# One-hot columns of an edge-count build: one two-input comparison for four windows, or two scalar comparisons for each

## The reference

```python
msgs = h[edge_src]
agg = jax.ops.segment_sum(msgs, edge_dst, num_segments=n) * inv_deg     # first network
deg = jax.ops.segment_sum(ones, dst, num_segments=n)                    # second network
mean = jax.ops.segment_sum(x[src], dst, num_segments=n) / clip(deg, 1.0)
```

## Time and profile before

| | |
|---|---|
| median of three runs | 639.3 us |
| the profiled execution | 638.31 us |
| its span, first to last instruction | 636.5 us |
| TensorE busy | 591.3 us, 93% |
| VectorE busy | 243.6 us, 38% |
| ScalarE busy | 219.3 us, 34% |
| GpSimd busy | 28.7 us, 5% |

### The profile page before, as it was taken

How to read it: one execution, slowest core, us unless ns; L and a number is a source line. 1 busy time by engine, 2 the same in 40 slices (tenths; PEclk the granted TensorE clock), 3 DMA queues, 4 the chain that set the end, 5 groups by cost and what they waited for, 6 DMA issues and landing times.

```text
span 636.5 us, 9707 instructions
## 1 busy us (share of the span) xinstructions
PE 591.3 (93%) x3133; PEld 348.6 (55%) x3133; DVE 243.6 (38%) x483; ACT 219.3 (34%) x391; POOL 28.7 (5%) x35
## 2 busy tenths in 40 slices
PE   0348999999999999999999999999999999999996
PEld 0336786868677656444545545654454545444455
DVE  5569885858576751476741111110010101000000
ACT  0466665656565542254542212211111111011112
POOL 2810000000000000001110000000000000000000
PEclk9999999999999999999999999999999999999999
DMA  9303000100000000432311000030020100101011
GB/s 228 91 11 93 0 17 2 33 1 32 0 32 16 18 20 23 129 97 88 82 33 42 16 16 16 5 91 16 1 49 0 44 5 18 31 6 42 0 37 27
DMA packets 28303, 23.97 MB, mean 38 GB/s; under 512 B 4783, under 2 KB 27618, under 8 KB 28149
## 3 DMA queue, kind: packets, MB, share of 16 engines
q1 hardware_dynamic: 23740, 20.49, 12.3%
q10 hardware_dynamic: 3337, 1.80, 1.4%
q0 software_dynamic: 1200, 1.33, 0.7%
HBM read 17.41 MB, written 6.19 MB: 37 GB/s over the span
## 4 chain that ended last, share of the span: by engine, by line
PE 89%; DMA 3%; POOL 2%; DVE 2%; issue 1%; ACT 1%; ACTq 0%; SPq 0%; DVEq 0%; POOLq 0%
PE ps L818 51%; PE ps L835 22%; PE ps L853 12%; PE ps L828 2%; DMA key_d<-adj 1%; POOL adj L1146 1%; PE ps L1039 1%; POOL adj L1158 1%; POOL adj L1152 1%; DMA invc<-inv_d 1%; DMA wt_d<-adj 1%; DMA adj<-key_d,adj 1%; PE ps L1011 1%; PE ps L1357 1%; DMA adj<-in_dst_dram 0%
## 5 line engine op out<-in xcount | busy, mean ns | idle before, releaser
L818 PE MATMUL ps<-adj,hs_b 125*128 (+2 forms) x1050 | 205.7, 352 | 0.0
L818 PE MATMUL ps<-adj,hs_a 125*128 (+2 forms) x700 | 162.4, 357 | 0.0
L818 PEld LDWEIGHTS ps<-adj,hs_b 125*128 125x128 f16 x1050 | 95.6, 97 | 105.8 <-issue 9.9
L475 DVE TENSOR_TENSOR hs_b<-iota,hs_b 128x1000 f16<-128x1000 f16 (+1 forms) x175 | 130.2, 797 | 40.5 <-PE ps L853 34.8
L680 ACT ACTIVATE adj<-ps 125x500 f32 (+3 forms) x175 | 98.2, 567 | 52.3 <-PE ps L853 47.5
L853 PEld LDWEIGHTS ps<-hs_b 128*125 128x125 f16 x625 | 94.9, 204 | 35.5 <-DVE hs_b L475 9.9
L853 PE MATMUL ps<-hs_b 128*125 128x125 f16 x625 | 103.6, 298 | 4.6 <-ACT adj L680 2.3
L818 PEld LDWEIGHTS ps<-adj,hs_a 125*128 125x128 f16 x700 | 69.8, 107 | 37.0 <-issue 5.0
L665 DVE TENSOR_TENSOR hs_a<-ps,hs_a 125x512 f32<-125x512 f32 (+1 forms) x7 | 4.4, 634 | 170.3 <-PE ps L1085 170.3
L835 PE MATMUL ps<-aggT,wts 128*128 128x500 f32 (+1 forms) x112 | 44.5, 540 | 0.4 <-ACT aggT L778 0.4
L835 PE MATMUL ps<-aggT,hs_a 128*128 128x500 f32 (+1 forms) x84 | 35.1, 540 | 0.5 <-ACT aggT L806 0.5
(11 more groups left out here) (143 smaller groups left out, 341.3 us busy)
## 6 DMA issues: line engine op xcount, KB each, us to landing
invc<-inv_d SPq DMA_DIRECT2D x24, 250.0 KB, 3.4
self_d<-hs_b SPq DMA_DIRECT2D x6, 250.0 KB, 2.0
hs_b<-self_d SPq DMA_DIRECT2D x6, 250.0 KB, 3.5
hs_b<-in_x_dram SPq DMA_DIRECT2D x6, 250.0 KB
x_d<-hs_b SPq DMA_DIRECT2D x6, 250.0 KB
hs_a<-x_d SPq DMA_DIRECT2D x6, 250.0 KB
out_dram<-hs_a SPq DMA_DIRECT2D x6, 250.0 KB
wt_d<-adj SPq DMA_DIRECT2D x1, 1152.0 KB, 4.1
```

Of the source, the lines that this page charges most:

```text
L475: last = nc.vector.tensor_tensor(onehots[slot][:, :, :, 0:nw], iota4[:, :, 0:nw].unsqueeze(1).to_broadcast(shape), keys[:, :, ds(win, nw)] ...
L818: last = nc.tensor.matmul(acc[:, 0:n], hs[:, ds(s * (2 * w) + part * w + h * 128, 128)], adj[0:P, ds(s * N + c * C, n)], start=(isinstance ...
```

## The change

Each group's single `tensor_tensor` becomes two `tensor_scalar` comparisons for each window: the iota of 128 values in consecutive f16 elements, compared with one key column of `kp` and then of `kn`, which is handed over as a scalar for each partition. A full group has eight such instructions in place of one; a group of the last chunk has two. The result is packed: each window's one-hot is 128 consecutive values, and so are the columns that the matmuls read. The weights become 128 columns wide (the last three are zero, as no key reaches 125) and the product has 128 rows; the moving operand stays at 125 columns. The iota tile is 128 values instead of 500, and slots, semaphores and order stay the same.

```diff
-        iota = sb("iota", P * GW, F16)
+        iota = sb("iota", 128, F16)
...
-        keys = kpn.rearrange("p (k n) -> p k n", k=2)
-        by_window = lambda t: t.rearrange("p (v w) -> p v w", w=GW)
-        onehots = [over(hs_b, up + 2560 + 2048 * i, 2 * P * GW, F16).rearrange("p (k v w) -> p k v w", k=2, w=GW)
+        onehots = [over(hs_b, up + 2560 + 2048 * i, 2 * 128 * GW, F16).rearrange("p (k w v) -> p k w v", k=2, w=GW)
                    for i in range(4)]
-        iota4 = by_window(iota)
...
                 win = g * GW if full else NFULL * S * GW + (g - NFULL * S)
-                shape = [128, 2, P, nw]
-                last = nc.vector.tensor_tensor(onehots[slot][:, :, :, 0:nw], iota4[:, :, 0:nw].unsqueeze(1).to_broadcast(shape),
-                                               keys[:, :, ds(win, nw)].unsqueeze(2).to_broadcast(shape), ALU.is_equal)
+                for w in range(nw):
+                    for k, key in enumerate((kp, kn)):
+                        last = nc.vector.tensor_scalar(onehots[slot][:, k, w, :], iota[:], key[:, ds(win + w, 1)], None, ALU.is_equal)
                 last.then_inc(sem("onehot"), 1)
...
-                    last = nc.tensor.matmul(bank(i % 2 if b is None else b)[0:P, w * WD * S:(w + 1) * WD * S], onehots[slot][:, 0, :, w],
-                                            onehots[slot][:, 1, :, w], start=True, stop=True)
+                    last = nc.tensor.matmul(bank(i % 2 if b is None else b)[:, w * WD * S:(w + 1) * WD * S], onehots[slot][:, 0, w, :],
+                                            onehots[slot][:, 1, w, 0:WD * S], start=True, stop=True)
...
-            nc.gpsimd.iota(iota4, [[1, P], [0, GW]], base=0, channel_multiplier=0,
+            nc.gpsimd.iota(iota[:], [[1, 128]], base=0, channel_multiplier=0,
```

## The result

The changed kernel takes 684.33 us (median of 4 runs, 683.22 to 685.16) against 639.24 us of the kernel before beside it (638.74 to 639.43): a ratio of 1.0706, 95% interval 1.0687 to 1.0724. It is slower by 45 us; the forecast was 674 us in 649 to 706. The profiled execution took 685.16 us with a span of 683.3, so its span is 46.8 us longer than before.

A forecast was written before the change was run, and what follows sets the result against it. VectorE bounds the prologue, TensorE the steps; VectorE would then bound all full groups. Prologue +13.8, step 0 +8.1, steps 1 to 4 +14.9, step 5 -1.5: +35.1 on 638.3, plus 1.0 to the median, 674 us, range 649 to 706.

The forecast's parts named there:

- VectorE becomes the bound of every stretch with full groups: Prologue and steps 0 to 4: VectorE's comparisons set the pace, with TensorE's shorter work beside them; +35.1 us in all.
- The pace: VectorE's time for one full group of four windows: 1.27 us by the sequencer, 0.84 to 1.36 by the datapath.
- The neighbours: Distance between successive TENSOR_SCALARs of the one-hots in the prologue: near 150 ns if the prediction is right.
- The sequencer's pair: VectorE's register operation plus handing over one comparison, done in turn: 129 to 152 ns, eight times for a full group.
- Prologue and step 0: The stretches before step 1, 25 groups each at VectorE's new pace: +13.8 us and +8.1 us.
- Steps 1 to 4: Each step becomes VectorE's 33.8 us against 30.05: +3.7 us each, +14.9 us together.
- No slot wait remains: Steps 1 to 4: in a dense block of 3.35 us VectorE fills three slots, 3.8 us, so it never waits.
- Step 5: Single windows: two comparisons stay under TensorE's piece, which falls by one matmul's 59 ns: -1.5 us.
- TensorE's gain: Count matmuls with 128 packed weight columns, priced at 56 ns in place of 115: 0.24 us less for a full piece.
- Rival A: Loop of build_c: sequencer and column scalar are hidden, 0.84 us a group; -25.6 us, or 614 us; 8%.
- Rival B: VectorE's comparisons: datapath waits for registers and scalar in turn, 1.5 us a group; +69.6, or 709 us; 7%.
- Rival C: TensorE, idle for half of every piece, falls back to its lower clock in steps 0 to 5; some 746 us; 5%.

The follow-up runs named there:

- e1: The changed kernel with each comparison's key column at a fixed address, so no address comes from a register: 684.63 us, ratio 1.0705 to the kernel before.
- e2: The changed kernel with a constant as scalar and the input's address from registers, so no per-partition scalar is read: 665.07 us, ratio 1.0403 to the kernel before.
- e3: The changed kernel with a constant as scalar and the iota as input, so neither registers nor column scalar: 625.16 us, ratio 0.9774 to the kernel before.
- e5: The changed kernel's packed layout and matmuls, but one two-input comparison makes each group's one-hots: 662.80 us, ratio 1.0362 to the kernel before.
- e8: The changed kernel with half of the terms of hidden1 and second1 left out, so dense blocks are shorter: 670.22 us, ratio 1.0475 to the kernel before.
- e9: The kernel before with packed one-hots, by one two-input comparison, only for the last chunk's single windows: 637.22 us, ratio 0.9969.
- e4: The kernel before with one-hots and weights widened from 125 to 128, stride of four kept in both operands: 639.78 us, ratio 1.0006.
- e7: The changed kernel with weights at a stride of four from one two-input comparison, moving operand packed by four scalar comparisons: 678.21 us, ratio 1.0599 to the kernel before.
- e6: The changed kernel with weights of 125 packed columns in place of 128: 685.13 us, ratio 1.0713 to the kernel before.

## Why the prediction was right, and where it was off

**VectorE becomes the bound of every stretch with full groups: right.** The windows show it busy for 34.30 of 34.30 us in step 0, and the waits of the count's weight loads for one-hots went to 14.1 us in one step. The 2.6 that I set against it is the sum of three steps, so the rise is larger than I wrote.

**The pace: 1.27 us forecast, 1.30 to 1.31 measured, and the reason was not the one I took.** I took the sequencer's. e1 shows that the datapath alone gives 1.30 and e2 that the sequencer alone gives 1.30 in the prologue. In the steps e2 is the faster, 33.0 us against 36.4, so there the datapath sets the pace; in the prologue the two come out equal. That a sum over the sequencer came within 0.04 us is in part luck. Of the terms, the datapath's 105 ns with a constant (102 measured) and 65 ns for the column scalar (60) were good; their sum, 8 x 170 = 1.36, is about as near to 1.30 as the 1.27 was. The neighbours, for which I had named 150 ns, stand 162.5 apart. The sequencer's pair was good too (130), but the loop's turn and the group's ends cost 0.78 us for three groups in e2, not the 0.16 of the page's three short rows.

**Prologue and step 0: +13.8 and +8.1 forecast.** The first aggregate came 15.8 us later. 0.95 of that is a later first one-hot, 48.17 in place of 47.22; across the kernels run it lay between 47.0 and 48.6, and I have no cause for it. The rest is g: 25 x 0.035 = 0.9. For the first dense block the forecast gives 13.8 + 8.1 + 7 x (1.27 - 0.88) = +24.6, and with the prologue's 2.0 and 32 x 0.035 = 1.1 for g it would be +27.7; measured are +27.0.

**Steps 1 to 4: +3.7 forecast, +6.2 to +6.6 measured. This step failed, in "No slot wait remains".** I set a dense block of 3.35 us against 3.8 us of work for three slots. The trace has 0.73 us and more of slot wait at each block, because the count's return takes longer than the block itself: by e3, e5 and the changed kernel together it is 4.6 to 4.7 us. With the block halved (e8) the waits are gone, except at one block that a fall of the clock had lengthened. Of the 2.6 us missed in a step 0.9 is g (25 x 0.035) and 1.5 to 2.4 the two waits, the most where the clock fell. That the slots are the cause rests on the trace, e3, e5 and e8; a kernel with more slots was not tried, and the four fill the space up to `selfT`.

**Step 5: -1.5 forecast, -1.4 measured.** This is the only gain of the change that reaches the time. By itself, in e9, it is 2.2 us (637.22 against 639.41 of the kernel before beside it).

The whole miss in span is 46.8 - 35.1 = 11.7 us: 150 x 0.035 = 5.2 for g, 7.0 for the eight slot waits (6 x 0.73 + 0.99 + 1.63), 0.95 for the start. This is 13.2, 1.5 more than there is. About 0.7 of that lies ahead of the first dense block (27.7 against 27.0), and 0.6 in the three other instructions of a step, which take 1.84 us and not the 2.0 of the sum; the last 0.2 is open.

**TensorE's gain: right in size, wrong in reason.** 57.5 ns forecast as 56. I had priced it by the weights; e4 and e7 show that most of it is the stride of the moving operand. Of the 54 ns between 111 and 57.5, e6 and e7 put some 13 on the width of packed weights and some 5 on their stride.

**Rival A** (faster, 614 us) stood or fell with the column scalar: e3, without it and without registers, is at 625 us. **Rival B** (1.5 us a group): sequencer and datapath do run beside each other, or the 130 and the 162 ns would add. **Rival C**, the clock: falls to 1.2 GHz came, but three times for 3.4 us each, not for whole steps. Where one meets count pieces alone it costs nothing, since TensorE has more than 6 us of idle time in a step. Where one reaches into a dense block, or ends as the block starts, the slot wait behind it grows, by 0.27 and 0.90 us here and by 1.6 and 0.9 in e1. That is 1.2 of the 46.8 us, and small against the 107 us that the rival had. Of the changed kernel's four runs two had a mean granted clock of 0.957 and 0.952 and took 683.95 and 684.71 us, two had 0.993 and 0.991 and took 685.16 and 683.22. These means do not speak of the short falls: the three of the profiled run leave 0.993. In e6, whose profiled run has 0.954, the difference is a stretch at 1.2 GHz from 37.2 to 88.4 us, in the prologue, where TensorE waits for VectorE in any case.

## What to carry to other kernels

Price a small VectorE instruction by the distance of neighbours of its own kind, operands included: 102 ns with a constant became 162 with a column, so that eight of them take 1.30 us where the one that they replaced took 0.72. Then look at what the sequencer does per instruction, and take the turn of the loop from a trace in which it is exposed. When the pace of a producer changes, work out the waits at every buffer anew with the consumer's whole absence (4.6 to 4.7 us here), not with the length of the block that causes it (3.35). And where a layout helps one engine and hurts another, it can be used for just as many tiles as the second has time for: the last chunk's groups gave 0.3% and 8 of 25 in the steps 0.4% more, where all of them, the prologue's too, cost 3.6% (e5).

## What the runs showed of the hardware that I had not expected

- A scalar read per partition costs 60 ns an instruction between back-to-back neighbours: 162.5 ns against 102 for 128 f16 values.
- A moving operand with a stride of four f16 values puts 110 to 115 ns between 125-column matmuls, packed 57.5; the same stride in the weights alone leaves 62 (e7).
- A weight load's duration (204, 156, 117, 105 ns) says little of the matmul's distance here: 110 ns with 117 (e4), 70 with 156 (e6).
- A fall of TensorE's clock costs time even where VectorE is the bound, if it reaches into or up to a dense block, during which the slots are not returned: waits of 0.99 and 1.63 us in place of 0.73, and of 2.20 and 1.53 in place of 0.59 (e1).
- A two-input comparison with one input that stands still innermost takes 1.135 us for 1024 f16 values (e5) and 0.60 for 512 (e7); with four keys innermost, 0.72 us for 1000.
- VectorE's sequencer needs 130 ns for a comparison with one address from a register, and 0.5 us more at the turn of the loop, where nothing covers it (e2).
